# Gated attention and quantised projection on one core: two row transposes are moved behind the f product, a PSUM bank changes hands, and the start-up repeats its idle transposes

## What is computed

```python
def reference(x, ctx_1024, g_xattn, g_ffn, w_q, b_q, w_k, b_k, w_v, b_v, w_o, b_o, weight, bias):
    x = x + jnp.tanh(g_xattn[0]) * _L0_xattn_ref(_layernorm(x), ctx_1024, ctx_1024, w_q, ...)
    x = x + jnp.tanh(g_ffn[0]) * _L0_ffn_ref(_layernorm(x), weight, bias)
    return x
```

## Time and profile before

| | us |
|---|---|
| median of three runs | 1389.93 |
| profiled execution | 1392.38 |
| its span | 1390.6 |
| TensorE busy | 1354.2 (97%) |
| VectorE busy | 1124.7 (81%) |
| GpSimd busy | 938.7 (68%) |
| ScalarE busy | 916.6 (66%) |

### The profile page before, as it was taken

One profiled execution on the slowest core, in us unless ns is written; L12 is line 12 of the kernel. 1 busy time (PEld: TensorE's weight loads), 2 busy tenths in 40 slices (PEclk: granted clock), 3 DMA queues, 4 the chain that ended last, 5 costly groups with the idle time before them and its releaser, 6 DMA issues.

```text
span 1390.6 us, 34895 instructions
## 1 busy us (share of the span) xinstructions
PE 1354.2 (97%) x10608; PEld 1198.5 (86%) x10608; DVE 1124.7 (81%) x4219; ACT 916.6 (66%) x2969; POOL 938.7 (68%) x1449
## 2 busy tenths in 40 slices
PE   7899999999999999999999999999999999999987
PEld 7788888898888888888888888888888889889865
DVE  5768888788888888888878878888888888888773
ACT  4667666667666666667666667666666666766661
POOL 1657776677676777676677676677677667767564
PEclk9999999999999999999999999999999999999998
DMA  8444344444444444434444434444444444443320
GB/s 253 118 112 107 103 111 124 118 129 107 109 109 120 124 128 117 107 101 119 121 126 123 108 99 115 126 119 124 110 106 109 126 118 128 110 116 99 88 62 31
DMA packets 181912, 159.10 MB, mean 114 GB/s; under 512 B 30176, under 2 KB 164320, under 8 KB 181728
## 3 DMA queue, kind: packets, MB, share of 16 engines
q1 hardware_dynamic: 181728, 156.88, 43.3%
HBM read 39.33 MB, written 16.78 MB: 40 GB/s over the span
## 4 chain that ended last, share of the span: by engine, by line
PE 59%; DVE 20%; SPq 9%; issue 5%; DMA 3%; ACT 1%; POOL 1%; DVEq 0%; ACTq 0%; POOLq 0%
PE proj L549 14%; PE proj L551 13%; PE proj L550 13%; SPq L380 9%; PE pT_ps L616 8%; DVE all_probs L891 5%; PE proj L632 3%; DMA k_stack<-k_lo 3%; DVE stats L899 3%; PE s_ps L605 3%; PE proj L660 2%; DVE all_probs L1028 2%; DVE k_lo L920 2%; PE s_ps L606 1%; DVE oT_lo L954 1%
## 5 line engine op out<-in xcount | busy, mean ns | idle before, releaser
L458 POOL TENSOR_TENSOR all_probs<-all_probs,rden 128x128 f32<-128x128 f32 (+1 forms) x1024 | 504.1, 514 | 347.5 <-DVE rden L949 346.5
L735 ACT ACTIVATE all_probs<-all_probs,neg_max 128x128 f32<-128x128 f32 (+1 forms) x1024 | 458.3, 449 | 242.4 <-DVE neg_max L891 242.2
L891 DVE CUSTOM_DVE_ANT_0 all_probs<-s_ps,causal 128x128 f32<-128x128 f32 (+1 forms) x1024 | 324.4, 354 | 144.2 <-PE s_ps L606 137.1
L616 PE MATMUL pT_ps<-ident,all_probs 128*128 128x128 f32 x1536 | 265.0, 282 | 9.9 <-POOL all_probs L458 7.2
L735 ACT ACTIVATION_READ_ACCUMULATOR all_probs<-all_probs,neg_max 128x1 f32 x1024 | 193.1, 189 | 0.0
L817 ACT ACTIVATE all_probs<-pT_ps 128x384 f32<-128x384 f32 x256 | 125.4, 490 | 87.4 <-PE pT_ps L616 87.2
L616 PEld LDWEIGHTS pT_ps<-ident,all_probs 128*128 128x128 f32 x1536 | 160.8, 142 | 25.2 <-issue 14.1
L549 PE MATMUL proj<-cT_hi,wk_hi 128*128 128x256 f32 x512 | 153.8, 300 | 1.4 <-DVE wk_lo L844 1.4
L605 PE MATMUL s_ps<-k_stack,q_stack 96*128 96x256 f32 x512 | 152.8, 299 | 2.1 <-DVE neg_max L891 2.0
L549 PE MATMUL proj<-aT_hi,wq_hi 128*128 128x256 f32 x512 | 151.0, 295 | 2.3 <-DVE aT_lo L943 2.3
L550 PE MATMUL proj<-cT_lo,wk_hi 128*128 128x256 f32 x512 | 142.7, 279 | 0.0
(11 more groups left out here) (119 smaller groups left out, 3607.9 us busy)
## 6 DMA issues: line engine op xcount, KB each, us to landing
k_stack<-k_hi SPq DMA_DIRECT2D x512, 64.0 KB, 2.0
q_stack<-q_hi SPq DMA_DIRECT2D x512, 64.0 KB, 2.1
xs_yz<-in_x SPq DMA_DIRECT2D x32, 512.0 KB, 5.2
k_stack<-k_lo SPq DMA_DIRECT2D x256, 64.0 KB, 2.0
q_stack<-q_lo SPq DMA_DIRECT2D x256, 64.0 KB, 2.1
out<-xs_yz SPq DMA_DIRECT2D x64, 256.0 KB, 2.3
c_quads<-in_ctx SPq DMA_DIRECT2D x124, 128.0 KB, 2.9
vs<-in_L_xattn_w_k SPq DMA_DIRECT2D x2, 512.0 KB, 5.8
```

Of the source, the lines that this page charges most:

```text
L458: last = nc.gpsimd.tensor_tensor(p, p, rden[:, sd, t, h:h + 1].to_broadcast([P, (1 + t) * P]), ALU.mult)
L616: last = nc.tensor.transpose(pT_ps[h % 2][:, m * P:(m + 1) * P], probs[:, h % P_RING, m * P:(m + 1) * P], ident[:, :])
L735: last = nc.scalar.activation(probs[:, h % P_RING, cols], probs[:, h % P_RING, cols], ACT.Exp, scale=-1.0, bias=neg_max[:, sd, t, h:h + 1] ...
L891: last = nc.vector.tensor_tensor_reduce(probs[:, h % P_RING, cols], s_ps[h % 2][:, cols], causal[:, (1 - t) * P:], 1.0, MASKED, ALU.add, A ...
```

## The change

The two lists UNITS and SLOT_PARTS are replaced by LAGS and SLOT_WORK, which names the units of every slot. The order that comes out is:

slot 0: q1 q1 q1; 1: dT0 q1 k0; 2: k0 k0 k0; 3: dT1; 4: f0 f0 f0; 5: f0 f1 f1; 6: f1 f1; 7: xT0 xT1 o0 o0; 8: o0 o0 o1; 9: o1 o1 o1; 10: q0 q0 q0; 11: q0; 12: v0 v0 v0 v0; 13: k1 k1 k1; 14: k1 v1 v1; 15: v1 v1.

So dT0, xT0 and xT1 stand directly behind a head's own transposes; f1's first part comes before xT0's, so f1 gets the bank of k0 and xT0 the bank of the av product; q0 ends in slot 11 and not in slot 10. The context's second turn is on DVE in slot 6 (before 8), with its high half on ACT in slot 7 and its low half on POOL in slot 8. At start-up 16 more transposes of the identity stand before the wait for w_k.

```diff
-UNITS = [("q", 1, 2), ("dT", 0, 4), ("k", 0, 1), ("dT", 1, 4), ("f", 0, 4), ("xT", 0, 1), ("f", 1, 4), ("xT", 1, 1),
-         ("o", 0, 3), ("o", 1, 3), ("q", 0, 1), ("v", 0, 1), ("k", 1, 1), ("v", 1, 1)]
-
+LAGS = {("q", 0): 1, ("q", 1): 2, ("k", 0): 1, ("k", 1): 1, ("v", 0): 1, ("v", 1): 1, ("o", 0): 3, ("o", 1): 3,
+        ("f", 0): 4, ("f", 1): 4, ("dT", 0): 4, ("dT", 1): 4, ("xT", 0): 1, ("xT", 1): 1}
+SLOT_WORK = ("q1 q1 q1", "dT0 q1 k0", "k0 k0 k0", "dT1", "f0 f0 f0", "f0 f1 f1", "f1 f1", "xT0 xT1 o0 o0", "o0 o0 o1",
+             "o1 o1 o1", "q0 q0 q0", "q0", "v0 v0 v0 v0", "k1 k1 k1", "k1 v1 v1", "v1 v1")
-WAKING = 12
+WAKING = (12, 16)
-SLOT_PARTS = (3, 3, 3, 1, 3, 4, 3, 3, 3, 3, 3, 1, 3, 3, 3, 2)
-TURN_SLOTS = (5, 8)
+TURN_SLOTS = (5, 6)
...
-            for _ in range(WAKING):
+            for _ in range(WAKING[0]):
                 nc.tensor.transpose(proj[BANKS - 1][:, 0:P], ident[:, :], ident[:, :])
...
             def transpose_weight(u, w, c):
 
+                if u == 0:
+
+                    for _ in range(WAKING[1]):
+                        nc.tensor.transpose(proj[BANKS - 1][:, 0:P], ident[:, :], ident[:, :])
```

More of the change, by code:

```diff
@@ L99, in live @@
         return not isinstance(b, int) or 0 <= b < B
[L101 to L104, removed]
+    usual = [(s, (name[:-1], int(name[-1]))) for s in range(SLOTS) for name in SLOT_WORK[s].split()]
+    assert all(sum(unit == u for _, u in usual) == PARTS[unit[0]] for unit in LAGS)
     work = {}
@@ L111, in fused_kernel @@
             for s, (kind, half) in LAST_O:
-                work.setdefault((i, s), []).extend((kind, half, i - lag_of[kind, half], p) for p in range(PARTS[kind]))
+                work.setdefault((i, s), []).extend((kind, half, i - LAGS[kind, half], p) for p in range(PARTS[kind]))
         else:
[L114 to L117, removed]
+            part_of = dict.fromkeys(LAGS, 0)
+            for s, unit in usual:
+                if live(i - LAGS[unit]):
+                    work.setdefault((i, s), []).append((*unit, i - LAGS[unit], part_of[unit]))
+                part_of[unit] += 1
     work[1, 0] = [("cT", half, 0, 0) for half in range(T)] + work.get((1, 0), [])
```

## The result

| | before | after |
|---|---|---|
| median of the runs (us) | 1389.66 (12 runs) | 1394.2 (12 runs) |
| ratio, 95% interval | | 1.0035 [1.0023, 1.0046] |
| profiled execution, its span (us) | 1392.38, 1390.6 | 1393.75, 1392.0 |
| first scores (us) | 45.33 | 43.66 |
| from them to the scores of batch 2 | 75.25 | 77.23 |

The change is 0.35% slower: 4.9 us by the ratio, between 3.2 and 6.4 by its interval. The forecast was 6.6 us faster, and 1394.2 us lies above the range, 1377 to 1391. The two profiled executions differ by 1.4 us only, because that of before was 2.7 us above its median. So the two traces show where time moved, and the medians by how much.

A forecast was written before the change was run, and what follows sets the result against it. TensorE, busy 97% of the span, was taken to bound the kernel, so only its waits and low clock could be won. -11.4 + 5.7 - 0.9 + 0 = -6.6 us, median 1383.3 us; 8-in-10 range 1377 to 1391.

The forecast's parts named there:

- The bank of f1: Slot 5: f1 would wait for k_lo, early enough, instead of oT_lo, so its whole wait goes: -11.4 us.
- What is late next: Slot 5: head 2's transposes wait for head 0's copy behind k_lo; k_lo later than each step's slack costs TensorE.
- q0's later end: Slot 11: q_lo 2.0 us later, delaying SyncE's stacking of k1; nine steps stall, 5.3 us, +5.7 us with interruptions.
- the 15 named: Sign to look for: SyncE's wait for k1 falls from 57.7 to below 15 us.
- interruptions: SyncE: interruptions that now fall in idle time, 0.4 us added to the cost of q0's later end.
- Transposes joined: dT0, xT0, xT1 put with other transposes: crossings cost next to nothing, 0.01 us each, -0.9 us in all.
- Moved work on POOL and the context: Slots 6 to 8: low halves and context turn moved; nothing on the path, up to +1 us if wrong.
- Start-up: Sixteen added transposes and the first steps: up to -2.5 us, then +1.5 us; net 0, between -2 and +3 us.
- the emptier stretch: First two steps with heads: less work while TensorE idles can hold the clock down longer, +1 to +3 us, +1.5 taken.
- The rival named for the slower side: q_lo 2.8 us later, so stalls outweigh the removed wait: +3.8 us, 1393.7 us; chance 0.08.

The follow-up runs named there:

- bank_alone: Kernel before with one edit: in slot 5 xT0 stands behind f1's two parts, so f1 takes k0's bank; 1388.6 us, ratio 0.9977 to before.
- q0_back: Changed kernel with q0's four parts and v0's first back where they were before the change, nothing else; ratio 0.998 to the kernel before.
- q0_late: Kernel before with q0 ending one slot later, in slot 11, all else as before; ratio 1.0076 to before, 10.5 us slower.
- late_k2_wake: Kernel before with k0's copy late (k_hi in slot 4 ahead of the exponentials, k_lo behind oT_lo, from step 4) plus the sixteen start-up transposes; ratio 0.9897 to before.

## Why the prediction was wrong

**The bank of f1: this step failed.** The prediction said that the wait for the bank "goes whole: -11.4 us". It was worth -3.2 us by the runs of bank_alone (-2.1 to -4.5), and -2.8 us worked out from the trace of before. The section looked up who held the new bank, `k_lo`, and found it early; it didn't ask for f1's other waits. The trace it had read gave the answer away: in the earlier trace rows `oT_lo` starts at 713.20 us directly behind `aT_lo`, which f1 needs as an operand and which was left out there (timeline of VectorE, kernel before):

```profile
712.62 0.67 DVE L943 TENSOR_TENSOR aT_lo<-proj,aT_hi 128x512 fp32r<-128x512 f32 x1
```

The next releaser was 0.6 us ahead, and 0.44 us of that were spent on f1's own earlier start.

**What is late next, and q0's later end: the mechanism right, the price about right.** `q_lo` ends 2.0 us later within the step on average (9.9 us ahead of head 0's scores before, 7.9 after), as said. SyncE's wait for k1 fell to 5.9 us, below the 15 named. The price was put at 5.3 us and 0.4 for interruptions; the traces of q0_back and the changed kernel give 5.6 us in the 29 steps and 0.9 ahead of batch 2, the runs 7.6 us in all. Only half of its place was right. Transposes do wait for the copy (6.1 us of the 13.9), but the larger part is f1 behind `aT_lo` (7.8 us), which is queued behind that same copy.

**An interruption right behind SyncE's last issue counts too.** The prediction reads k_stack's lateness from the issues of k1. In 22 of the 29 steps of the kernel before `k_hi` starts 2.1 to 2.2 us behind the last of the twelve issues, whenever that comes. In the other seven the last issue is on time, 7.2 us behind head 0's scores, and `k_hi` starts 2.9 to 3.4 us behind it; these seven steps hold 5.2 of the 11.3 us. The step of the earlier trace rows is one of them: last issue at 706.02, `k_hi` at 709.40. SyncE's next four issues, those of the context, are longer in it than in a step that doesn't wait (timeline of SyncE, kernel before, the step from 575.34 us and then that from 698.81):

```profile
582.55 0.60 SPq L380 DMA_DIRECT2D k_stack<-k_lo  x1
583.19 2.09 SPq L370 DMA_DIRECT2D c_quads<-in_ctx  x4
```

```profile
706.66 3.24 SPq L370 DMA_DIRECT2D c_quads<-in_ctx  x4
```

Six of the seven steps load a context, and in all six its issues take 2.5 to 3.2 us; in the 22 others they take 2.1, but for one with 2.5. So what holds SyncE up there seems to hold the DMA just issued as well. That is read from two things that go together, and no run tests it.

**Transposes joined: right, and nothing.** Steps without a wait went from 40.97 to 40.95 us: 29 x 0.02 = 0.6 us, where 0.9 was said. The other 15 slots together, with 0.43 us of xT0's moved into them in each step, went from 1099.7 to 1112.2 us: 12.5 us more, and 29 x 0.43 = 12.5.

**Moved work on POOL and the context: right.** No wait of line 619 for POOL between 150 and 1300 us.

**Start-up: the sum near, its parts no firmer than one execution.** The first scores came 1.7 us earlier and the next two steps took 2.0 us more, where -1.5 and +1.5 were said. The second half has q0 in it: q0_late alone adds 2.3 us there, and q0_back takes back 0.9. The prediction put it down to the emptier stretch and the clock. The first half is within what executions of one start-up differ by. That the added transposes run at the raised clock is right (below).

With -3.2 in place of -11.4 the same sum gives -3.2 + 5.7 - 0.9 + 0 = +1.6 us, 1391.5 us; 1394.2 was measured. With q0's place at the 7.6 us of the runs and the transposes at -0.6 it is +3.8 us, inside the measured 3.2 to 6.4. So one term was wrong by 8 us and one small by about 2. The rival named for the slower side (SyncE late by 2.8 us) was not the mechanism: 2.0 us were enough, since there was little gain to outweigh.

## What to carry over

When a wait is to be removed, list everything the waiting instruction needs, operands and bank, with the time of each, and subtract from the gain how much earlier it will then want to start; what is gained is the distance to the second releaser, not the wait. Where several late operations stand in a row on one engine, look for the first that waits for something far away: here the k unit's copy, held by DMAs, pushed everything queued behind it, and putting it one slot later, behind that work, gained what moving the last link couldn't. To settle which of two releasers counts, swap them. Before a gain of 1 or 2 us is read from one trace, look how far traces of the same instructions differ.

## What the runs showed of the hardware

**The clock at start-up differs between executions of one instruction list.** bank_alone and the kernel before have the same start-up. In bank_alone the granted clock reached 1.00 at about 4.9 us; in that of before the first row that shows it raised is at 17.98 us. k0's matmuls show which is which: in bank_alone they start 0.12 us apart (timeline of TensorE),

```profile
13.70 0.28 PE L549 MATMUL proj<-cT_lo,wk_hi 128*128 128x256 f32 x1
13.81 0.28 PE L550 MATMUL proj<-cT_hi,wk_lo 128*128 128x256 f32 x1
```

and 0.21 us apart in the kernel before. The stretches of the profile print a granted clock of 1.00 before the first change that they have, also where transposes start 0.22 us apart (1.8 to 8.6 us in the kernel before), so at the very start these distances are the reading. Of the five traces without the sixteen transposes two run all of k0 at 0.12 us a matmul (bank_alone, q0_late), and in the other three 13 to 19 of its 23 distances are 0.21 us. The prediction took the low clock there for a property of the kernel; it holds in some executions and not in others.

**Transposes alone raise the clock and run at it.** In the changed kernel TensorE had done nothing but transposes when the clock rose at 6.2 us, and in the eight other traces with the sixteen it rose at 5.5 to 7.5 us, likewise. In the changed kernel the sixteen took 1.75 us to the next start, 0.11 us each, where the first twelve had 0.22. Timeline of TensorE, then the stretches around it (us, busy of PE, PEld, DVE, ACT, POOL, granted clock, DMA share, GB/s):

```profile
1.81 2.82 PE L543 MATMUL proj<-ident 128*128 128x128 f32 x12 [1.81 <-POOL ident L447]
...
6.41 1.91 PE L568 MATMUL proj<-ident 128*128 128x128 f32 x16
8.16 1.12 PE L585 MATMUL s_ps<-ident,vs 128*128 128x128 f32 x8
```

```profile
6.20:13.00 6.80, 5.04 (x43) 4.84 (x42) 4.84 (x8) 3.05 (x6) 0.00 (x0) 1.00 1.02 279
13.10:16.40 3.30, 3.30 (x17) 3.30 (x17) 1.47 (x6) 0.82 (x3) 0.71 (x1) 0.50 0.98 337
```

This speaks, as the earlier trace rows did, against the rule of the Trainium skill that the full clock doesn't engage for transposes (page "TensorE: Matmul & The Clock Gate", section "Part 4: PE-mode transpose"). The Trainium skill speaks there of a transpose mode; the rows show a MATMUL with the identity, and not whether that mode is on. The clock fell again at 13 us, behind a pause of 1.76 us in which TensorE waited for w_k's low half; nine of k0's matmuls stood between the two. In six more of the nine traces it fell in the same way, at 12.3 to 13.6 us; in late_k2_wake and q0_back k0 ran at the full clock to its end. So waking TensorE ahead of w_k doesn't by itself keep it awake through k0.

**SyncE's issues are now and then much longer.** Two issues usually take 1.24 us; in the changed kernel a pair takes 2.67 us. Timeline of SyncE:

```profile
540.26 1.24 SPq L379 DMA_DIRECT2D k_stack<-k_hi  x2
541.55 0.60 SPq L379 DMA_DIRECT2D k_stack<-k_lo  x1
542.18 2.67 SPq L379 DMA_DIRECT2D k_stack<-k_hi  x2
```

Such interruptions fall in different steps, among or right behind the twelve issues, and slot 5 is long where `k_hi` is late. That is why slot 5 differs from step to step as long as the chain from SyncE ends on TensorE.
